# Bf16 parts in a selective scan, quadratics for a logarithm, and the distances of an alignment stored from another queue

## The reference, cut to what matters

```
# stage 1, selective scan; d 512, n 64, L 32, 32 sequences
delta = softplus(dt_raw)                   # [b, t, d]
for t in range(L):
    dA = exp(delta_t[..., None] * A)       # A = -exp(A_log)
    h  = dA * h + (delta_t * u_t)[..., None] * B_t[:, None, :]
    y_t = einsum('bdn,bn->bd', h, C_t)

# stage 3, alignment, per sequence: small = layernorm(x) [32, 256], large = ctx [257, 256]
D = sqrt(max(|s|^2 + |l|^2 - 2 s.l, 0))    # [32, 257]
R[i, j] = D[i, j] + min(R[i-1, j], R[i, j-1], R[i-1, j-1])
path back from the last cell (diagonal first, then up, then left)
x += for each token, the sum of the context rows on its path
```

## Time and profile before

| | us |
|---|---|
| median of 3 runs | 1982.43 |
| the three runs | 1971.89, 1982.43, 1983.95 |
| profiled execution | 1974.1 |
| its span | 1972.3 |
| lead-in and end outside the span | 1.8 |
| PE matmul busy | 1718.4 (87%) |
| VectorE busy | 1035.5 (52%) |
| ScalarE busy | 736.2 (37%) |
| POOL busy | 713.7 (36%) |
| preparation of the scan, first scan matmul | 384 to 464 |
| scan | 464 to 1058 |
| alignment stage | 1403 to 1554 |

### The profile page before, as it was taken

One profiled execution on the slowest core, in us unless ns is written; L12 is line 12 of the kernel. 1 busy time (PEld: TensorE's weight loads), 2 busy tenths in 40 slices (PEclk: granted clock), 3 DMA queues, 4 the chain that ended last, 5 costly groups with the idle time before them and its releaser, 6 DMA issues.

```text
span 1972.3 us, 24066 instructions
## 1 busy us (share of the span) xinstructions
PE 1718.4 (87%) x8919; PEld 828.1 (42%) x8936; DVE 1035.5 (52%) x1526; ACT 736.2 (37%) x1187; POOL 713.7 (36%) x428
## 2 busy tenths in 40 slices
PE   7888886996999999999998759999821979899998
PEld 4666653552322222322224535444410456654443
DVE  3444443177888888888884333222249464521121
ACT  2333332154676666666661221111312240112121
POOL 1333330214998998998994010000200005000000
PEclk9999997897999999999998758999865879789999
DMA  2111101011000000100100500110063100101110
GB/s 72 32 32 32 32 22 51 0 49 54 8 17 7 26 14 7 28 12 6 29 6 16 221 0 1 32 48 32 3 141 72 32 1 1 43 0 43 43 43 21
DMA packets 36488, 65.61 MB, mean 33 GB/s; under 512 B 13508, under 2 KB 22616, under 8 KB 34980
## 3 DMA queue, kind: packets, MB, share of 16 engines
q1 hardware_dynamic: 36404, 64.49, 11.1%
HBM read 55.80 MB, written 8.67 MB: 33 GB/s over the span
## 4 chain that ended last, share of the span: by engine, by line
PE 78%; DVE 14%; ACT 2%; DMA 2%; issue 2%; POOL 1%; SPq 1%; DVEq 0%; ACTq 0%; POOLq 0%
PE ps L813 15%; PE ps L854 7%; PE ps L827 6%; PE ps L1298 6%; PE ps L2059 6%; PE ps L2070 6%; PE ps L201 4%; PE ps L1311 3%; PE ps L342 3%; PE ps L347 3%; PE ps L224 2%; DVE arena L992 2%; PE ps L360 2%; DVE arena L477 2%; PE ps L1834 2%
## 5 line engine op out<-in xcount | busy, mean ns | idle before, releaser
L1078 POOL TENSOR_TENSOR arena<-arena 128x768 f32<-128x768 f32 x248 | 521.5, 2122 | 65.4 <-DVE arena L1030 42.8
L813 PE MATMUL ps<-arena 32*128 32x512 f32 x2016 | 330.7, 644 | 18.0 <-DVE arena L999 18.0
L1030 DVE TENSOR_TENSOR arena<-arena,ps 128x1024 f32<-128x1024 f32 x248 | 302.0, 1218 | 10.8 <-POOL arena L1078 4.4
L813 PEld LDWEIGHTS ps<-arena 32*128 32x128 f32 x2016 | 118.2, 184 | 223.8 <-issue 204.4
L940 ACT ACTIVATE arena<-arena 128x1024 f32<-128x1024 f32 x124 | 131.1, 1057 | 164.7 <-DVE arena L1010 164.7
L1010 DVE TENSOR_TENSOR arena<-arena,ps 128x1024 f32<-128x1024 f32 x124 | 151.4, 1221 | 78.2 <-PE ps L813 78.1
L854 PE MATMUL ps<-arena 128*32 128x512 f32 (+15 forms) x1024 | 136.2, 604 | 8.6 <-DVE arena L1030 8.0
L827 PE MATMUL ps<-arena 64*128 64x512 f32 x496 | 140.9, 645 | 0.0
L947 ACT ACTIVATE arena<-ps 128x1024 f32<-128x1024 f32 x124 | 127.0, 1024 | 19.1 <-PE ps L813 3.0
L1298 PE MATMUL ps<-arena 128*128 128x512 f32 x288 | 131.9, 602 | 1.1 <-ACT arena L1363 0.6
L949 ACT ACTIVATE arena<-arena 128x1024 f32<-128x1024 f32 x124 | 131.1, 1057 | 4.0
(11 more groups left out here) (288 smaller groups left out, 2412.8 us busy)
## 6 DMA issues: line engine op xcount, KB each, us to landing
arena<-ctxT SPq DMA_DIRECT2D x32, 257.0 KB, 3.0
arena<-ctxT SPq DMA_DIRECT2D x8, 1028.0 KB, 15.5
arena<-L_ffn_w SPq DMA_DIRECT2D x16, 512.0 KB, 4.2
arena<-ctx_rows SPq DMA_DIRECT2D x8, 960.0 KB
m_rows<-arena SPq DMA_DIRECT2D x16, 256.0 KB, 2.5
arena<-m_rows SPq DMA_DIRECT2D x64, 64.0 KB
arena<-L_ffn_eW SPq DMA_DIRECT2D x8, 512.0 KB, 3.6
m_yd<-arena SPq DMA_DIRECT2D x64, 32.0 KB, 2.3
```

Of the source, the lines that this page charges most:

```text
L813: mm = nc.tensor.matmul(ps[:, bank + jj, :], weights[r], m_row[r, n // CH % 2, n % CH, :], start=start, stop=True)
L1030: nc.vector.tensor_tensor(m_h[:, u, n % 2], m_xa[:, u, n % 2], ps[:, bank:bank + 2, :], ALU.add).then_inc(S["m_use"], 1)
L1078: nc.gpsimd.tensor_tensor(x, x, m_h[:, u, (n - 1) % 2].rearrange("p j d -> p (j d)")[:, own], ALU.mult).then_inc(S["m_kept"], 1)
```

## The change

Stage 1. The constant log A is split into three bf16 parts (`m_al[0..2]`) by VectorE, `m_id2` becomes bf16, and the logs of a step are six bf16 matmuls in place of two fp32 ones. The logarithm of softplus is a product of five quadratics: ACT makes each square (`square`), VectorE multiplies five times. The order of the preparation changes on PE and ACT: step sizes and B come out of one product ahead, C's products and B's transposes move behind the first `m_dudone`, the transposes of A move ahead, the evictions of the second convolution lie between the squares. `keep_b` on SP waits, as before, for `m_bev`, which now comes later. `m_du`, `m_al` and `m_Bc` move in memory.

Stage 3. ACT squares all eight tiles, ahead of all roots; POOL does none. The tokens' norms are computed by VectorE from `n_r`, the reciprocal of the layernorm's deviation (two instructions of 128x8). PE waits for the square only ahead of the norms of a tile. Each store of the distances is issued from ACT's queue behind its root, SP's queue only reloads, and `ctx_rows` wait for all reloads. `up` is made by ACT as the complement of a bf16 mask `stay`, and `dg` and `lf` are bf16 products and differences.

The diff, cut to its core (the names of semaphores, memory areas and the functions around are left out):

```diff
@@ m_pe
+            conv(0)
+            steps_and_b(0)
...
+            for c in range(IC):
+                mm = nc.tensor.transpose(ps[:, 6, c * P:(c + 1) * P], m_a2[:, c].rearrange("p s n -> p (s n)"), ident)
+            mm.then_inc(S["m_eat"], 1)
...
+            step_sizes(0)
+            conv(1)
+            u_by_token(0)
+            steps_and_b(1)
+            step_sizes(1)
+            for h in range(NH):
+                pe.wait_ge(*S.at("m_dudone", h + 1))
+                spread_c(h, bank_of(0, h))
...
+            u_by_token(1)
+            for n in range(8):
+                if n == 0:
+                    pe.wait_ge(*S.at("m_dudone", 4))
+                elif n < 3:
+                    pe.wait_ge(*S.at("m_cev", 2 * n))
+                elif n == 3:
+                    pe.wait_ge(*S.at("m_bev", 2))
+                else:
+                    pe.wait_ge(*S.at("mz_ev", n - 3))
...
             def logs(n):
                 bank = room(("l", n))
-                for jj in range(2):
-                    r = slice(NS * jj, NS * jj + NS)
-                    nc.tensor.matmul(ps[:, bank + jj, :], m_id2[r].rearrange("p s n -> p (s n)"), m_al[r], start=True, stop=False)
+                for part in range(3):
+                    for jj in range(2):
+                        r = slice(NS * jj, NS * jj + NS)
+                        nc.tensor.matmul(ps[:, bank + jj, :], m_id2[r].rearrange("p s n -> p (s n)"), m_al[part][r],
+                                         start=(part == 0), stop=False)
                 spread(bank, sel, n, 1, start=False)
@@ m_act
+            def square(h, k):
+                if k >= 2:
+                    act.wait_ge(*S.at("m_quad", 5 * h + k - 1))
+                nc.scalar.activation(m_sq(h, k), m_e[:, 4 * h:4 * h + 4], ACT.Square, scale=LOG1P_SCALE,
+                                     bias=m_bias[:, k:k + 1]).then_inc(S["m_sqd"], 1)
...
+            parts(0)
+            square(0, 0)
+            square(0, 1)
+            convolved(1, 0)
+            square(0, 2)
+            for c in range(1, IC):
+                convolved(1, c)
+            square(0, 3)
+            square(0, 4)
+            steps_and_b(1)
+            parts(1)
+            square(1, 0)
+            square(1, 1)
+            spread_c(0)
+            square(1, 2)
+            spread_c(1)
+            act.wait_ge(*S.at("m_alev", 1))
+            b_by_token(0)
+            b_by_token(1)
+            square(1, 3)
+            square(1, 4)
             logged(0)
@@ m_dve
-                ch.link(nc.vector.tensor_scalar(p, e, LOG1P[-1], None, ALU.mult))
-                for k in range(len(LOG1P) - 2, 0, -1):
-                    ch.link(nc.vector.scalar_tensor_tensor(out=p, in0=p, scalar=LOG1P[k], in1=e,
-                                                           op0=ALU.add, op1=ALU.mult))
...
+                for k, (_, left) in enumerate(LOG1P):
+                    n = 5 * h + k + 1
+                    dve.wait_ge(*S.at("m_sqd", n))
+                    nc.vector.scalar_tensor_tensor(out=p, in0=m_sq(h, k), scalar=left, in1=p if k else e,
+                                                   op0=ALU.add, op1=ALU.mult).then_inc(S["m_quad"], 1)
@@ d_load
-            keep(0)
-            for g in range(1, TT):
-                keep(g)
-                back(g - 1)
-            back(TT - 1)
-            sp.wait_ge(*S.at("d_ab", TT))
+            for g in range(TT):
+                sp.wait_ge(*S.at(f"d_out{g % 4}", 16 * (g // 4) + 16))
...
+            sp.wait_ge(*S.at("d_back", 16 * SEG * TT))
@@ d_pe
-            tile(0)
-            pe.wait_ge(*S.at("d_tsq", 1))
             for g in range(TT):
-                for k in range(DC):
-                    mm = nc.tensor.matmul(ps[:, 4, g:g + 1], U[2][:, k, g * P:(g + 1) * P], ones[:, 0:1],
-                                          start=(k == 0), stop=(k == 1))
-            mm.then_inc(S["d_bb"], 1)
-            for g in range(1, TT):
                 tile(g)
@@ d_act
+            deviation(0)
             squares(1)
...
+            deviation(1)
+            for g in range(2, TT):
+                squares(g)
+
+            for g in range(TT):
                 root(g)
+                if g >= 4:
+                    act.wait_ge(*S.at(f"d_out{g % 4}", 16 * (g // 4)))
+                act.wait_ge(*S.at("d_sqrt", 2 * g + 2))
+                act.dma_start(dist[:, g * P:(g + 1) * P].rearrange("k p i -> p k i"), d_dt[g]).then_inc(S[f"d_out{g % 4}"], 16)
...
+            act.wait_ge(*S.at("d_sort", 1))
+            nc.scalar.activation(by_slot(2)[:, :, 1:WW], d_stay[0:PB, :, 1:WW], ACT.Copy, bias=1.0,
+                                 scale=-1.0).then_inc(S["d_up"], 1)
@@ d_dve
-            dve.wait_ge(*S.at("d_bb", 1))
-            ch.link(nc.vector.tensor_copy(d_bb, ps[:, 4, 0:TT]))
+            ch.link(nc.vector.tensor_tensor(d_bb, n_r, n_r, ALU.mult))
+            ch.link(nc.vector.tensor_scalar(d_bb, d_bb, -D * 1e-5, float(D), ALU.mult, ALU.add))
...
+            ch.link(nc.vector.tensor_tensor(dg[:, :, own], dg[:, :, own], stay[:, :, own], ALU.mult))
+            ch.link(nc.vector.tensor_tensor(lf[:, :, own], stay[:, :, own], dg[:, :, own], ALU.subtract))
+            dve.wait_ge(*S.at("d_up", 1))
@@ d_pool
-            for g in range(ACT_SQ, TT):
-                nc.gpsimd.tensor_tensor(d_sq[g], d_ctx[g], d_ctx[g], ALU.mult).then_inc(S["d_ss"], 1)
```

More of the change, by code:

```diff
@@ L602, in build, with m_sq @@
         m_Btok = view(TAIL + 2208, TT, NS)
-        m_id2 = view(TAIL + 2720, SEQS, NS)
+        m_id2 = bview(TAIL + 2720, SEQS, NS)
         m_tiny = view(TAIL + 2848, 1)
         m_back = view(TAIL + 2849, P // 16, 16)
-        m_al = view(EXTRA, DI)
+        m_al = [bview(TAIL + 1696, DI), bview(TAIL + 1952, DI), bview(SM + 1024, DI)]
+        m_left = view(TAIL + 2208, DI)
+        m_bias = view(TAIL + 2977, 5)
+        m_Bc = view(25 * K, T)
+        m_du = [view(EXTRA, 4, DI)[:, q] for q in range(4)] + [view(24 * K, 4, DI)[:, q] for q in range(4)]
         FRONT = 30
+        def m_sq(h, k):
+            return view((6 if h else 10) * K + 2048 * (k % 2), 4, DI)
         CH = 8
@@ L733, in m_pe, with conv @@
             pe.wait_ge(*S.at("m_taps", IC * KW))
-            for h in range(NH):
+            def conv(h):
                 for c in range(IC):
@@ L774, in m_pe @@
                     mm.then_inc(S["mu_mm"], 1)
-            for h in range(NH):
-                for i in range(4):
-                    if h == 0:
-                        pe.wait_ge(*S.at("m_dudone", i + 1))
-                    else:
-                        pe.wait_ge(*S.at("mz_ev", i + 1))
-                    product(bank_of(0, i), P, [(m_win[:, k, (IC + i) * P:(IC + i + 1) * P], half(U[2], k, h))
-                                               for k in range(DC)], "mz_mm")
+            conv(0)
@@ new lines, in m_pe @@
+            step_sizes(1)
+            for h in range(NH):
+                pe.wait_ge(*S.at("m_dudone", h + 1))
+                spread_c(h, bank_of(0, h))
+            pe.wait_ge(*S.at("m_dudone", 3))
+            pe.wait_ge(*S.at("m_dtev", 4))
+            for h in range(NH):
+                for q in range(4 * h, 4 * h + 4):
+                    mm = nc.tensor.transpose(ps[:, bank_of(0, 2), q * NS:(q + 1) * NS], m_Bc[NS:P, q * P:(q + 1) * P],
+                                             ident[NS:P, NS:P])
+                mm.then_inc(S["m_bmm"], 1)
@@ new lines, in m_pe @@
+            u_by_token(1)
[8 more added lines that the diff above has]
+                    pe.wait_ge(*S.at("mz_ev", n - 3))
+                product(bank_of(0, (n + 3) % 4), P, [(m_win[:, k, (IC + n % 4) * P:(IC + n % 4 + 1) * P], half(U[2], k, n // 4))
+                                                     for k in range(DC)], "mz_mm")
@@ L921, in m_act, with spread_c, b_by_token @@
                 nc.scalar.activation(m_e[:, 4 * h:4 * h + 4], m_e[:, 4 * h:4 * h + 4], ACT.Exp, scale=-1.0).then_inc(S["m_e"], 1)
+                act.wait_ge(*S.at("m_e", h + 1))
+            def square(h, k):
[3 more added lines that the diff above has]
+                                     bias=m_bias[:, k:k + 1]).then_inc(S["m_sqd"], 1)
+            def spread_c(h):
+                act.wait_ge(*S.at("m_cmm", h + 1))
+                per = PAIRS // NH
+                for s in range(SEQS):
+                    r = slice(NS * s, NS * s + NS)
+                    nc.scalar.copy(m_C[r, FRONT + h * per * L * SEQS:FRONT + (h + 1) * per * L * SEQS]
+                                   .rearrange("p (j t s) -> p j t s", t=L, s=SEQS)[:, :, :, s],
+                                   ps[r, bank_of(0, h), :].rearrange("p (j s t) -> p j s t", s=SEQS, t=L)[:, :, s, :]).then_inc(S["m_cev"], 1)
+            def b_by_token(h):
+                act.wait_ge(*S.at("m_bmm", 2))
+                nc.scalar.copy(m_Btok[:, 4 * h:4 * h + 4].rearrange("p q n -> p (q n)"),
```

(13 more changed lines are left out.)

137 lines of the change are left out of this document (60 added, 77 removed).

## The result

| | before | after |
|---|---|---|
| median, us | 1983.19 (4 runs, 1971.89 to 1986.32) | 1950.45 (4 runs, 1949.09 to 1953.92) |
| profiled execution, us | 1974.1 | 1953.92 |
| its span, us | 1972.3 | 1952.1 |

The ratio is 0.9847, 95% interval 0.9825 to 0.987: 32.7 us between the medians, where the terms of the forecast add up to -33.6. The profiled pair differs by 20.2 us only, and the stages show where. Each length is a difference of two starts on PE or VectorE.

A forecast was written before the change was run, and what follows sets the result against it. The scan was taken as bound by the loop through VectorE, not PE. Preparation -18.1, alignment -14.0, masks -1.5 and scan 0 sum to -33.6 us: 1940.5 from the profiled run, 1948.8 from the median, middle 1945, range 1932 to 1966.

The forecast's parts named there:

- The scan: Scan steps: bf16 logs free PE 0.10 us a step, but the loop through VectorE sets the step: 0 us.
- Rival (a): Scan: PE was its pace after all, so 124 steps gain 0.10 us each, -12.7 us, 1932; chance 0.07.
- (b): Scan logs: a bf16 pass costs what an fp32 pass does, 0.53 us; 57 us lost, 2002; chance 0.05.
- four signs named: Scan: step 4.56 us, read-out 0.06 behind the state, logs about 0.96, weight queue idle about 0.9 ahead of the read-out.
- The preparation: Before the scan: reordered work and ScalarE squares let PE's first scan matmul start 16.6 us earlier, at 447.6, released by reloads.
- The clock: Scan's first fills: a shorter PE standstill may keep the clock high, worth up to 3 us, half counted.
- The alignment: Distance stage: earlier roots and stores moved off SyncE start the forward pass at 1446.1, -14.0 us, bounds -17 to -9.8.
- 3.5 + 4.5: Alignment: assumed times from last root through last store's and last reload's landings to the forward pass, 8.0 us together.
- variant of the forecast: Alignment: stores still meet reloads on shared DMA engines, landing in 5.0 and 6.1 us; -10.9, about 1948; chance 0.2.
- The masks: Alignment masks: steps of 3.20, 3.20 and 1.70 us become one of 3.20 and two of 1.70, -1.5 us.
- (c): A new wait, costly store issue on ScalarE or late chunk landing, leaves -24 or so, 1954; chance 0.13.
- (d): Preparation held by an unseen link (z products, table load, B's late store); half the total goes, 1962; chance 0.08.

The follow-up runs named there:

- s1: The changed kernel with the scan's logs put back to two fp32 matmuls: 1948.75 us, ratio 0.9839.
- s8: The changed kernel with fp32 logs and each half of the read-out waiting only for its own state: 1948.36 us, ratio 0.9846.
- a3: The changed kernel with distances in 96-column DRAM rows, so reloads are 128 packets, and SyncE's preparation stores reordered, Ln rows last: 1956.57 us, ratio 0.9884.
- s4: The changed kernel with the stores of the distances back on SyncE's queue, in turn with the reloads: 1957.22 us, ratio 0.9877.
- a1: The changed kernel with each distance reload written as rows of 348 bytes; the packets stayed as they were: 1952.16 us, ratio 0.9854.
- a2: The changed kernel with each row of a distance reload written in four parts; the packets stayed as they were: 1953.77 us, ratio 0.9863.
- s3: The changed kernel with fp32 logs and the read-out moved behind drive 1, ahead of the logs: 2042.23 us, ratio 1.031.
- s5: The changed kernel with the read-out moved to the end of PE's step, behind the bf16 logs: 2038.61 us, ratio 1.0301.
- s6: The changed kernel with fp32 logs and the read-out moved to the end of PE's step: 2080.07 us, ratio 1.0495.
- s7: The changed kernel, bf16 logs, with each half of the read-out waiting only for its own state: 1947.32 us, ratio 0.9833.
- s9: The changed kernel with the read-out's first half between logs and their broadcast, and SyncE's preparation stores reordered, Ln rows last: 2007.99 us, ratio 1.0125.
- s2: The changed kernel with the read-out moved behind drive 1, ahead of the bf16 logs: 2001.70 us, ratio 1.0108.

## Why the prediction was right, and where its terms were not

**The scan, 0 us: right, and by the step as put.** The rate, the second state and the read-out follow each other as before, 4.56 us, and s1 with fp32 logs is no slower. PE's spare time with fp32 logs was 0.07 by the forecast and is 0.08 by s8. But the reading was incomplete: the loop through VectorE is one of three bounds within 0.08 us. What I did not see is the ring: the wait of drive 0 for the rate. Rival (a) falls, and so does (b), since a pass costs 0.76 / 3 = 0.25 us against the 0.32 that I took and the 0.53 of (b), which loses from 0.378 on. Of the four signs named, the step and the 0.06 came out; the logs took 0.76 and not 0.96, and the weight queue's idle time ahead of the read-out stayed 0.83 where 0.9 was forecast, because PE's gain went into the wait for the rate. I had taken the idle time ahead of one instruction for all of PE's room.

**The preparation, -16.6 forecast, -15.3 measured.** The ten further kernels with the same order of stores took 78.0 to 78.4 us. Shifted by the 4.3 us by which the convolution began later, the steps came out as worked: first exponentials at 402.47 (402.4), quadratics of the second half until 439.90 (439.9), the first Ln until 439.1 (439.15), z until 450.91 (449.3). The reloads' landing was the mis-sized term: 4.99 us in place of 3.7. (The cold end of the stated bounds is a slip: 464.2 - 450.0 is 14.2 and not 13.5.) The step "z or the chunk" went as forecast, with the chunk last; a3 shows that z is only 2.2 us behind. 

**The clock, -1.5 us (half of 3): not gained.** The granted clock (PEclk, the number ahead of the last two) of the changed kernel and of s1 in windows of 4 us from the start of the scan:

```profile
449.00:453.00 4.00, 1.27 (x3) 0.20 (x2) 0.00 (x0) 2.85 (x5) 0.00 (x0) 1.00 0.25 53
453.00:457.00 4.00, 3.83 (x20) 1.49 (x22) 1.22 (x1) 2.89 (x3) 0.00 (x0) 0.74 0.99 310
457.00:461.00 4.00, 4.00 (x16) 1.04 (x12) 3.10 (x3) 2.96 (x3) 1.82 (x1) 0.50 0.68 253
461.00:465.00 4.00, 4.00 (x20) 0.71 (x16) 2.04 (x3) 1.40 (x3) 2.39 (x1) 0.50 0.10 38
```
```profile
453.00:457.00 4.00, 3.85 (x16) 1.48 (x18) 1.22 (x1) 2.95 (x4) 0.00 (x0) 0.75 1.00 317
457.00:461.00 4.00, 4.00 (x20) 1.19 (x18) 3.27 (x3) 2.87 (x3) 1.82 (x1) 0.82 0.65 241
461.00:465.00 4.00, 4.00 (x28) 1.01 (x24) 2.87 (x4) 2.35 (x3) 3.55 (x2) 1.00 0.11 41
```

PE had stood still for 2.9 and 2.8 us and begun the scan at 2.4 GHz (1.00 up to 453), as forecast for a warm start. Then the clock fell to 1.2 GHz in both; in s1 it was back at 2.4 in the next window, in the changed kernel only after 465. The changed kernel's second read-out of the scan came 15.8 us after the first scan matmul, in s1 13.3, and before, from a cold start, 15.0. Four profiles are of kernels with the preparation and the scan of the change: the lower clock lasted some 10 us in the changed kernel, s4 and a1 and 14 in a2, which began the scan with it after a standstill of 2.5 us; their second read-outs came at 15.8, 15.8, 15.8 and 17.3 us. Where a program differed it was shorter: 3 to 4 us with another order or other logs in the scan (s1, s3, s5, s6, s7) or another order of stores (s9, a3), and none in s2 and s8. So the term is nothing here: the second read-out even came 0.8 us later than from the cold start before. What decides between 10 and 3 us isn't shown. The 1.5 us by which the stretch from the first scan matmul to the alignment got shorter are not this term: the scan itself took 589.0 us before and 590.3 after.

**The alignment, -14.0 forecast, -7.3 measured, -8.9 by the mean of eleven profiles (-7.1 to -11.0): the term most in error, in most of them outside its bound of -9.8.** The roots came earlier as forecast: the last store was issued 32.9 us into the stage, against 34.9 forecast for the last root. Wrong was "3.5 + 4.5", the landings: from the last store's issue to the forward pass 16.7 us went by, and 12.3 to 14.9 in the ten other kernels, in place of 8.0. The chain shows 10.55 for the store and 6.15 for the reload. Two errors lie in this. The reload's 4.5 was too small from the start: the last one before took 5.99, and the last store 4.98, so before's own landings would have given some 11 us. The rest is the stores: while they overlap with the reloads they land later, the slowest in 7.7 to 10.6 us in the eleven kernels, against 6.1 before and 6.8 in s4. For the last reload no change is clear: 6.15 us here and 4.5 to 7.7 in the ten others, 5.99 before. The Trainium skill, DMA: Bandwidth & Descriptors, section Issuing engines are not separate DMA queues, says that DMAs of different issuers run on the same 16 engines and interleave. The trace agrees in the direction: with the stores on ScalarE's queue their landing has a median of 6.8 us in the changed kernel and 5.5 to 6.3 in the ten others (on SyncE's, before and in s4, 5.0). It does not agree that only the time of issue is saved, since s4 loses 6.3 us. In s4's chain four landings stand one behind another on SyncE's queue: stores in 6.81, 4.99 and 4.94 us and the last reload in 4.39. Such waits, and not the time of issue, were most of what the move took away. The variant of the forecast that I had put at 0.2 gave -10.9 and was the nearer one.

**The masks, -1.5: -1.3.** Forward pass to next stage, 93.93 to 92.68, and in s1, s7 and s8 92.6 to 92.7.

**Rivals (c) and (d)** did not occur as put: 0.37 us for an issue on ScalarE, and no unseen link in the preparation. The chunk did land 1.3 us late, and the terms as measured, -25.5, lie nearer to the -24 of (c) than to -33.6.

**The sum.** -15.3, -8.9 and -1.3 are -25.5. The medians differ by 32.7. Some 7 us of the medians' difference are not in the terms; that before's only profile was a quick execution covers them in size, but no stage shows it. The forecast of 1945 was 5 us low; the term of the alignment is 5 us too large. So that the sum of -33.6 comes within 1 us of the -32.7 of the medians is luck: the terms as measured give 7 us less. What was right is the mechanism of the scan and of the preparation.

**What stays open.** What sets the landing of 6 to 10 us when stores and reloads overlap: it is not the long packets (a3), and s4 changes the queue and the overlap at once, so it doesn't separate them. In the changed kernel the packets of both queues took 31% of the engines' time from 1410 to 1442 (17.5 and 13.1%, the first with some of the `ctx_rows`), so on average most of it was unused. No kernel here beats the changed one by more than the error: s7 at 1947.32 lies 3 us below it, and the order of SyncE's stores gives 2.0 us in its own stage (a3, s9) but was not run without another change beside it.

## What to carry to other kernels

A loop found by following one engine is one of several. Where buffers form a ring, write out for each fill which reader frees its buffer, add up that loop too, and compare all of them before a reorder is priced; here three lay within 0.08 us. Two reorders ran into the ring at a new place, and the third into PE's own work, whose half read-outs had been priced at half. An edit is worth what the loop contains of it: the same bf16 logs gave 0 us in one order and 40 us in two others. And when transfers are freed from waiting for each other, their landing times must be priced for the overlap that this makes, and never below what the trace of before shows for the same transfer.

## What the hardware showed that was not expected

- A bf16 pass on two row groups of 512 columns cost 0.25 us (0.76 for three), less than the 0.32 extrapolated from 257 columns.
- Four matmul records of the read-out cost PE 0.98 us, eight 0.97: matmuls to different column groups of the array overlap, so removing half of them from a group saves nothing, and putting them elsewhere costs all of it again (s9, +0.5 us a step).
- Two broadcasts on different row groups take 1.2 us together, one alone 1.05 (s5, 804.15 to 805.20). The orders of s2 and s5 part such a pair and pay for a broadcast alone.
- A reload of 128 rows of 348 bytes from rows of 384 cost SyncE 0.60 to 1.95 us to issue, one of 4 long packets 0.29; a store of 384 rows of 348 bytes cost ScalarE 0.37.
- After a standstill of 2.9 us PE began at 2.4 GHz and fell to 1.2 GHz 1.7 us into the scan, while it was busy. It stayed there some 10 us. In s1, whose logs are fp32, it was 3 to 4 us, and the second read-out came 2.5 us sooner.
